# One layer of cross attention finished by the tile, and self attention with its output step moved one pipeline step later

## The chip, the cores and the metric

The kernel runs on one core of one Trainium2 chip. The core has TensorE (PE, matrix products and transposes into PSUM), VectorE (DVE), ScalarE (ACT), GpSimd (POOL) and SyncE (SP, here only for DMAs). Each engine works through its own instructions in order, and they meet through semaphores. The metric is the device time of one execution in microseconds; lower is better. Everything is computed in float32.

## What is computed

A small perceiver of two layers: 128 sequences of 32 latents with 128 features, and a context of 257 rows a sequence. Each layer is a cross attention to the context, a self attention and a mixture of eight experts (two a token), with residuals and norms between. Cut to the parts that the change touches, the reference computes:

```python
# layer 1, cross attention, 16 heads of 8, per sequence
q = z(x) @ Wq.T; k = ctx @ Wk.T; v = ctx @ Wv.T
p = softmax(q k^T / sqrt(128))          # 32 x 257 a head
x = x + (p @ v) @ Wo.T + bo
# self attention of both layers, 16 heads of 8, 32 x 32 scores a head
x = x + (softmax(scores) @ v) @ Wo      # layer 0 relative positions, layer 1 causal with rotary factors
# then a router picks two of eight experts for each token
```

## The kernel before

The work stands in passes, one after another with a barrier between. A tile is 128 tokens, that is 4 sequences (B4) of 32 latents (LEN); there are 32 tiles.

`cross_many_heads` (the second cross attention, semaphores p6) works in units of one sequence, 4 a tile, 128 in all, as a software pipeline: in one step b the engines have several units in hand. For one unit b:

- PE makes the scores (L1493, 4 groups of 4 heads, 257 columns), then in the same step the keys and values of the unit two later (L1501, L1503), the transposes of the probabilities of the unit before (L1514), and for the unit two back the transposes of `spread` (L1533, in `shares`) and the product of values and probabilities (L1540, in `weigh`).
- DVE takes the negated row maxima (L1633, in `largest`), then a copy of the last probability column and the reciprocal of the sums (L1673, L1674), a copy of half the turned probabilities (L1678), and `finish` of the unit three back: `end_ps` times the last value (L1614), plus `o_ps` (L1617), times `share_ps` (L1621), and a sum over the 4 heads of a group into `oT` (L1625). `finish` stands ahead of `largest`.
- ACT makes the exponentials (L1586, four a unit, each with a read of its sum), the copy of keys and values (L1595) and the other half of the turned probabilities (L1602). The next scores wait for the last exponential.
- POOL spreads the last column and the reciprocals over the heads (L1720, 128 x 256), and does the norms and the joining of the experts' results for other tiles.

Softmax has 257 columns; the 257th (`LAST`) is handled apart from the 256 that are turned, with `m.last_values`.

Once a tile, in steps of their own: b=0 the normed input (L287, L1562), b=1 its copy and the query product (L1651, L1564), b=2 the queries (L1656) and the output product (L1567), b=3 the residual (L1664). `joined.dve` ends DVE's step 1 and `tail.dve` its step 3.

`self_attention` serves both layers (p4 relative, p8 causal). Here a step is a whole tile, and step n has tile n - s at stage s: 0 norm and transpose (`zT`), 1 queries and keys, 2 values, 3 scores, sum, maximum, subtraction (POOL L1375) and exponential (ACT L1253), 4 transpose of the probabilities (DVE L1327), the weighted values (PE L1211, here called weigh) and the division (`o`, DVE L1350, L1352), 5 transpose of `o` (PE L1171), its copy (ACT L1234), the output product (PE L1184) and the new X (DVE L1341). `Routing` runs in the same steps with a lag of READY: norms of a group of four tiles (POOL L264), router logits, the choice (DVE L938 to L972), ranks, and the scatter of the rows to the experts' input (POOL L776). STEPS is 32 + AFTER. The order inside a step is written out by hand: PE scores, queries and keys, transpose of `o`, values, output product, transpose of z, router work, weigh; ACT keys and queries, copy of `oT`, `zT`, exponential, copy of the values (`v_all`, L1262), rows for the experts. ACT's copy of the values may overwrite a buffer only when the weighted values of two tiles before are done.

Of the kernel before, what the change touches and what calls it, by code (L numbers as in the profile page):

```python
# [24 lines left out]
P = 128  # L25
# [660 lines left out]
class Routing:  # L686
# [6 lines left out]
    READY = 8  # L693
    AFTER = 18
# [74 lines left out]
    def pool_scatter(self, pool, n, k):  # L769
        m, s = self.m, self.s  # L770
        g, j = self.group_at(n, 9, self.GROUP)
# [107 lines left out]
    def act_slots(self, act, n):  # L879
        s = self.s  # L880
        g, j = self.group_at(n, 9)
# [23 lines left out]
    def dve_logits(self, dve, n, weighed):  # L905
        s = self.s
        g, j = self.group_at(n, 4)
# [66 lines left out]
    def dve_place(self, dve, n, weighed):  # L974
        s = self.s
        g, j = self.group_at(n, 8)
# [90 lines left out]
def self_attention(m, name, relative):  # L1067
# [20 lines left out]
    with ExitStack() as own, nc.Block() as block:  # L1088
# [4 lines left out]
        v_all = sb("v_all", [P, 2, B4 * G, H4, HD + 1])  # L1093
# [45 lines left out]
        def _(pe):  # L1139
            mm = nc.tensor.matmul  # L1140

            def work(n, at):
                t = at(3)
                if t.live:
# [4 lines left out]
                    if t.past(3):  # L1149
                        pe.wait_ge(tail.x_new, t.before(3))  # L1150
# [14 lines left out]
                t = at(5)  # L1165
                if t.live:
                    pe.wait_ge(s["o"], t.nth())
                    if at(1).live:
                        pe.wait_ge(s["zT"], at(1).nth())
                    routing.pe_turned_read(pe, n)  # L1170
                    nc.tensor.transpose(oT_ps, o[:, t.par, :], ident).then_inc(s["oT_ps"], 1)  # L1171
# [7 lines left out]
                t = at(5)  # L1179
                if t.live:  # L1180
                    pe.wait_ge(s["oT"], t.nth())
                    if at(3).live:
                        pe.wait_ge(s["summed"], at(3).nth())
                    mm(y_ps, oT[:, t.par, :], wo, start=True, stop=True).then_inc(s["y_ps"], 1)  # L1184
# [20 lines left out]
                if t.live:  # L1205
                    pe.wait_ge(s["pT"], t.nth())
                    pe.wait_ge(s["v"], t.nth(H4))
                    for b in range(B4):
                        for g in range(G):
                            w, n = H4 * (HD + 1), b * G + g  # L1210
                            last = mm(o_ps[b * LEN:(b + 1) * LEN, g * w:(g + 1) * w],  # L1211
                                      pT[:, t.par, n * LEN:(n + 1) * LEN], v_all[:, t.par, n],
# [6 lines left out]
        def _(act):  # L1219
            def work(n, at):  # L1220
                routing.act_slots(act, n)
                t = at(1)
# [6 lines left out]
                t = at(5)  # L1229
                if t.live:  # L1230
                    act.wait_ge(s["oT_ps"], t.nth())
                    if t.past(2):
                        act.wait_ge(s["y_ps"], t.before(2))
                    nc.scalar.activation(oT[:, t.par, :], oT_ps, ACT.Copy).then_inc(s["oT"], 1)  # L1234
# [19 lines left out]
                t = at(2)  # L1254
                if t.live:
                    act.wait_ge(s["v_ps"], t.nth())
                    act.wait_ge(s["ones"], 3)
                    if t.past(2):
                        act.wait_ge(s["o_ps"], t.before(2))
# [148 lines left out]
def cross_many_heads(m):  # L1408
# [22 lines left out]
    with ExitStack() as own, nc.Block() as block:  # L1431
# [174 lines left out]
        def _(dve):  # L1606
# [29 lines left out]
            def steps(at):  # L1636
                cur, nxt, prev = at(3), at(2), at(4)
                for b in range(B4):
# [6 lines left out]
                    if t.live:  # L1645
                        finish(t, u)
# [423 lines left out]
```

## Time and profile before

| | us |
|---|---|
| median of 3 runs | 1639.16 (1632.37 to 1641.44) |
| the profiled execution | 1640.08 |
| its span in the trace | 1638.1 |

| engine | busy us | share |
|---|---|---|
| PE matmul | 1280.6 | 78% |
| PE weight load | 1107.7 | 68% |
| DVE | 1093.9 | 67% |
| ACT | 840.1 | 51% |
| POOL | 771.2 | 47% |

The busy shares are means over passes with different limits. In time order the passes are: setup and first cross attention to 175 us, relative scores to 207, the first self attention to 466, the first experts to 637, the second cross attention to about 1213, the second self attention to about 1460 with its tables, the second experts and the joining of their results to the end. A row of the timeline gives start, duration, engine, line, operation, output and input, and in square brackets the idle time before it with what ended it. The clock column of the windows is TensorE's granted clock as a share of 2.4 GHz; 0.50 is 1.2 GHz.

### The profile page before, as it was taken

The page shows a single profiled execution, that of the slowest core. Times are in us where ns is not written, and L with a number is a line of the kernel's source. Part 1 is how long each engine was busy: PE and PEld are TensorE (multiplying, and loading weights), DVE is VectorE, ACT ScalarE, POOL GpSimd, SP SyncE. Part 2 cuts the span into 40 slices and gives each one's busy share as a digit, 9 for nine tenths or more (in the row PEclk, how much of TensorE's full clock was granted, in tenths as well). Part 3 has the DMA queues.
Part 4 walks back from the last instruction along what each step waited for, and adds up shares of the span by engine and source line. Part 5 has one row for each costly group of instructions (what it writes and reads, how often), then busy time and mean ns, then how long its engine had stood idle before and what let it go on. Part 6 is the DMA issues. An engine that isn't in the chain of part 4 may idle for free. (4 is left out here: it accounts for less than half of the span.)

```text
span 1638.1 us, 48674 instructions
## 1 busy us (share of the span) xinstructions
PE 1280.6 (78%) x15138; PEld 1107.7 (68%) x15139; DVE 1093.9 (67%) x3599; ACT 840.1 (51%) x2658; POOL 771.2 (47%) x1508
## 2 busy tenths in 40 slices
PE   3878789897659995888888888888869898529991
PEld 2656778786659994666666666666648787529991
DVE  4555377877356663888888888888868977523334
ACT  1554256564224442666666666666646756315440
POOL 2555033767546653444443444444333465646661
PEclk9898588888579997999999999999978989659996
DMA  7997552221122212121111111111000000022225
GB/s 224 254 251 196 207 166 69 60 60 50 36 63 67 63 53 89 60 66 67 32 32 48 32 32 44 36 32 32 27 14 2 10 22 25 32 61 72 68 59 164
DMA packets 91996, 122.00 MB, mean 74 GB/s; under 512 B 12689, under 2 KB 67218, under 8 KB 91858
## 3 DMA queue, kind: packets, MB, share of 16 engines
q1 hardware_dynamic: 74194, 82.77, 17.3%
q0 software_dynamic: 12288, 34.82, 7.3%
q10 hardware_dynamic: 5376, 2.63, 0.5%
q8 instruction: 80, 1.31, 0.3%
q14 instruction: 58, 0.48, 0.1%
HBM read 89.68 MB, written 30.49 MB: 73 GB/s over the span
## 5 line engine op out<-in xcount | busy, mean ns | idle before, releaser
L1586 ACT ACTIVATE p_prob<-six,p_nm 128x257 f32<-128x257 f32 x512 | 235.9, 474 | 187.4 <-DVE p_nm L1633 180.5
L1720 POOL TENSOR_TENSOR p_spread<-p_both,sb_const 128x256 f32<-128x256 f32 x128 | 78.4, 613 | 248.1 <-DVE p_both L1674 190.5
L1633 DVE TENSOR_REDUCE p_nm<-six 128x2 f32<-128x514 f32 x256 | 164.7, 684 | 10.2 <-PE six L1493 4.8
L1493 PE MATMUL six<-p_kv,p_q_all 32*128 32x257 f32 x1024 | 92.2, 426 | 94.7 <-ACT p_prob L1586 94.5
L1823 PE MATMUL bank<-sb_w,m_experts_aT 128*128 x1152 | 155.7, 278 | 6.9 <-ACT m_experts_aT L1852 4.4
L1839 PE MATMUL six<-m_experts_xT,m_experts_w 128*128 128x128 f32 x1152 | 156.0, 279 | 0.1
L1802 POOL DMA_INDIRECT expert_outputs<-m_experts_y,m_experts_dest x144 | 142.6, 990 | 26.1 <-POOL m_experts_tiny L1801 14.7
L1823 PEld LDWEIGHTS bank<-sb_w,m_experts_aT 128*128 128x128 f32 x1152 | 140.4, 192 | 11.9 <-issue 11.7
L776 POOL DMA_INDIRECT expert_inputs<-p_r_x,p_r_slot x128 | 126.2, 986 | 41.6 <-issue 34.0
L1839 PEld LDWEIGHTS six<-m_experts_xT,m_experts_w 128*128 128x128 f32 x1152 | 143.3, 196 | 0.7 <-issue 0.3
L1514 PE MATMUL six<-sb_const,p_prob 128*128 128x128 f32 x1024 | 138.1, 280 | 1.8 <-ACT p_pT L1602 1.6
L1375 POOL TENSOR_TENSOR p_score<-p_score,p_mx 128x512 f32<-128x512 f32 x64 | 67.0, 1048 | 153.4 <-DVE p_mx L1320 151.6
L1493 PEld LDWEIGHTS six<-p_kv,p_q_all 32*128 32x128 f32 x1024 | 43.5, 184 | 124.6 <-issue 124.6
L1514 PEld LDWEIGHTS six<-sb_const,p_prob 128*128 128x128 f32 x1024 | 120.9, 145 | 2.7 <-ACT p_prob L1586 1.8
L1678 DVE COPY p_pT<-six 128x512 f32<-128x512 f32 x128 | 86.4, 675 | 38.7 <-PE six L1514 38.7
L1586 ACT ACTIVATION_READ_ACCUMULATOR p_prob<-six,p_nm 128x1 f32 x512 | 104.0, 203 | 0.0
L1154 PE MATMUL six<-p_kT,p_q_all 32*128 32x32 f32 x2048 | 87.5, 286 | 7.1 <-issue 5.3
L1801 POOL TENSOR_TENSOR m_experts_tiny<-sb_const 128x1 f32<-128x1 f32 x144 | 40.1, 278 | 111.7 <-DVE m_experts_y L1880 59.4
L1501 PE MATMUL bank<-p_ctxT,sb_w_WkT_x 128*128 128x256 f32 x256 | 92.1, 442 | 0.8 <-ACT p_kv L1595 0.8
L1595 ACT ACTIVATE p_kv<-bank 128x512 f32<-128x512 f32 x128 | 77.9, 608 | 24.1 <-PE bank L1503 24.1
L1154 PEld LDWEIGHTS six<-p_kT,p_q_all 32*128 32x128 f32 x2048 | 77.6, 199 | 14.6 <-issue 11.5
L1262 ACT ACTIVATE p_v_all<-bank 32x128 f32<-32x128 f32 x256 | 70.6, 276 | 31.6 <-PE bank L1211 19.3
(282 smaller groups left out, 3404.4 us busy)
## 6 DMA issues: line engine op xcount, KB each, us to landing
ctxN_ring<-ctxN POOLq DMA_DIRECT2D x32, 516.0 KB, 11.3
ctxT_ring<-ctxT SPq DMA_DIRECT2D x32, 514.0 KB, 12.0
p_ctxT<-ctxT SPq DMA_DIRECT2D x32, 514.0 KB, 3.6
m_experts_x<-expert_inputs SPq DMA_DIRECT2D x144, 64.5 KB
bd_scores<-p_rows SPq DMA_DIRECT2D x32, 256.0 KB, 2.8
p_bd<-bd_scores SPq DMA_DIRECT2D x32, 256.0 KB
sb_w<-w SPq DMA_DIRECT2D x32, 256.0 KB
p_y<-expert_outputs SPq DMA_DIRECT2D x32, 128.0 KB, 3.5
```

Of the source, the lines that this page charges most:

```text
L776: m.nc.gpsimd.indirect_dma_start(m.xs_dram[:, :], bass.IndirectOffsetOnAxis(ap=self.slot[:, TOPK * t + k:TOPK * t + k + 1], axis=0), self. ...
L1154: last = mm(quad[:, g, keys], q_all[rows, t.par, b], kT[rows, t.par, keys], start=True, stop=True, tile_position=(32 * g, 0))
L1493: last = mm(scores_ps[:, g, 0:CTX], q_all[rows, t.par, b], kT[rows, t.par, b, :], start=True, stop=True, tile_position=(32 * g, 0))
L1501: mm(ps[6][:, 0:LAST], m.w["WkT_x"][:, :], ctxT[:, t.par, b, 0:LAST], start=True, stop=True)
L1514: last = nc.tensor.transpose(turned_ps[g // 2][:, g % 2, n * P:(n + 1) * P], prob[:, b, g, n * P:(n + 1) * P], ident)
L1586: last = nc.scalar.activation(prob[:, b, g, :], scores_ps[:, g, 0:CTX], ACT.Exp, bias=nm[:, b % 2, g:g + 1], accum_out=total[:, b % 2, g:g ...
L1633: nc.vector.tensor_reduce(nm[:, b % 2, g:g + 2], scores_ps[:, g:g + 2, 0:CTX], AX.X, ALU.max, negate=True).then_inc(s[most], 1)
L1678: nc.vector.tensor_copy(pT[:, u % 2, 2:4], turned_ps[1]).then_inc(s["pT_b"], 1)
L1720: nc.gpsimd.tensor_tensor(spread[:, u % 2], both[:, u % 2].rearrange("p k g -> p (k g)").unsqueeze(2).unsqueeze(3).broadcast_to([P, 2 * G, ...
L1802: nc.gpsimd.indirect_dma_start(m.ys_dram[:, :], bass.IndirectOffsetOnAxis(ap=dest[:, t.par:t.par + 1], axis=0), y[:, t.par, :], None).then ...
L1823: last = nc.tensor.matmul(ps[6 + t.two][:, 0:D], aT[:, t.two, f * P:(f + 1) * P], m.w2[:, DS(held[p] + f * D, D)], start=(f == 0), stop=(f ...
L1839: last = nc.tensor.matmul(ps[2 + t.two][:, f * P:(f + 1) * P], w[:, t.two, f * P:(f + 1) * P], xT[:, t.two, :], start=True, stop=True)
```

## The change

In the cross attention `finish` becomes one copy of `share_ps` and one product `o_ps` times that copy, which goes to a tile-wide buffer `masked`; the sum over the four heads moves to POOL, once a tile, as two additions (`halves`, then `oT`). The 257th column is no longer added on DVE in each unit: POOL makes the spread in two operations (share, then share times the last probabilities), PE sums it over the latents' group with a small product into `end_ps`, DVE multiplies it by the last values once a tile (`end_v`), and a second output product adds it. `finish` now stands first in DVE's step. In the self attentions the transpose of `o`, its copy, the output product and the new X go from stage 5 to stage 6, the division from the end of DVE's step (stage 4) to the start of the next (stage 5); the transpose of `o` stands first in PE's step, its copy first in ACT's; ACT copies the values ahead of `zT` and the exponential, and the values have three buffers. READY and AFTER grow by one.

```diff
@@ Routing
-    READY = 8
-    AFTER = 18
+    READY = 9
+    AFTER = 19
@@ self_attention, buffers
-        v_all = sb("v_all", [P, 2, B4 * G, H4, HD + 1])
+        v_all = sb("v_all", [P, 3, B4 * G, H4, HD + 1])
@@ PE: now first in the step, ahead of the scores (was stage 5, behind queries and keys)
+                t = at(6)
+                if t.live:
+                    pe.wait_ge(s["o"], t.nth())
+                    if at(1).live:
+                        pe.wait_ge(s["zT"], at(1).nth())
+                    routing.pe_turned_read(pe, n)
+                    nc.tensor.transpose(oT_ps, o[:, t.par, :], ident).then_inc(s["oT_ps"], 1)
@@ ACT: copy of oT first; then keys, queries; then the values; then zT, exponential
+                t = at(6)
+                if t.live:
+                    act.wait_ge(s["oT_ps"], t.nth())
...
+                t = at(2)
+                if t.live:
+                    act.wait_ge(s["v_ps"], t.nth())
+                    act.wait_ge(s["ones"], 4)
+                    if t.past(3):
+                        act.wait_ge(s["o_ps"], t.before(3))
@@ DVE: the division at the start of the next step, with dve_logits and dve_place
+                t = at(5)
+                if t.live:
+                    dve.wait_ge(s["o_ps"], t.nth())
...
@@ cross_many_heads, PE
-                for out, first in ((share_ps, 0), (end_ps, G)):
-                    nc.tensor.transpose(out, spread[:, b % 2, first:first + G].rearrange("p g h d -> p (g h d)"), ident)
+                nc.tensor.transpose(share_ps, spread[:, b % 2, 0].rearrange("p g h d -> p (g h d)"), ident)
+                mm(end_ps[:, b * LEN:(b + 1) * LEN], spread[:, b % 2, 1].rearrange("p g h d -> p (g h d)"),
+                   c[:, C_R4:C_R4 + LEN], start=True, stop=True)
...
-                        pe.wait_ge(s["oT"], seq(prev, B4 - 1))
-                        mm(misc_ps, oT[:, prev.par, :], m.w["WoT_x"][:, :], start=True, stop=True).then_inc(s["y_ps"], 1)
+                        pe.wait_ge(s["oT"], prev.nth())
+                        mm(misc_ps, oT[:, prev.par, :], m.w["WoT_x"][:, :], start=True, stop=False)
+                        mm(misc_ps, end_v[:, prev.par, :], m.w["WoT_x"][:, :], start=False, stop=True).then_inc(s["y_ps"], 1)
@@ DVE
-                nc.vector.tensor_scalar(ended[:, :], end_ps, m.last_values[:, n:n + 1] if t.known else ...
-                nc.vector.tensor_tensor(whole[:, :], o_ps, ended[:, :], ALU.add).then_inc(s["whole"], 1)
-                nc.vector.tensor_tensor(shared[:, :], whole[:, :], share_ps, ALU.mult).then_inc(s["shared"], 1)
-                nc.vector.tensor_reduce(oT[:, t.par, b * LEN:(b + 1) * LEN], ...
+                nc.vector.tensor_copy(share[:, b % 2, :], share_ps).then_inc(s["share"], 1)
+                nc.vector.tensor_tensor(masked[:, t.par, :, b * LEN:(b + 1) * LEN], o_ps..., share[:, b % 2, :]..., ALU.mult)
+                    if b == 2 and prev.live:
+                        nc.vector.tensor_tensor(end_v[:, prev.par, :]..., end_ps..., m.last_values[:, prev.cols(B4)]..., ALU.mult)
-                        nc.vector.tensor_copy(both[:, u % 2, 1, :], prob[:, u, :, LAST]).then_inc(s["ends"], 1)
@@ POOL
+                    if b == 2 and prev.live:
+                        pool.wait_ge(s["masked"], seq(prev, B4 - 1))
+                        nc.gpsimd.tensor_tensor(halves[:, :, :], masked[:, prev.par, 0:2, :], masked[:, prev.par, 2:4, :], ALU.add)
+                        pool.wait_ge(s["halves"], prev.nth())
+                        nc.gpsimd.tensor_tensor(oT[:, prev.par, :], halves[:, 0, :], halves[:, 1, :], ALU.add)
-                        nc.gpsimd.tensor_tensor(spread[:, u % 2], both..., mine, ALU.mult).then_inc(s["spread"], 1)
+                        nc.gpsimd.tensor_tensor(spread[:, u % 2, 0], recip..., mine, ALU.mult).then_inc(s["spread_share"], 1)
+                        nc.gpsimd.tensor_tensor(spread[:, u % 2, 1], spread[:, u % 2, 0], prob[:, u, :, LAST]..., ALU.mult)
```

## Rows read from the trace of the kernel before

**Rows 1.** Windows by pass: first self attention, second cross, second self.
```profile
207.00:447.00 240.00, 200.42 (x2770) 182.14 (x2770) 164.97 (x558) 130.36 (x353) 131.60 (x202) 0.78 0.25 74
645.00:1213.00 568.00, 468.42 (x5261) 369.04 (x5257) 486.17 (x1522) 373.02 (x1279) 236.16 (x614) 0.98 0.13 41
1222.00:1416.00 194.00, 167.61 (x2669) 151.47 (x2669) 152.08 (x526) 115.98 (x302) 98.87 (x139) 0.87 0.06 18
```
**Rows 2.** Timeline of one tile of the second cross attention, steps b=0 to b=3.
```profile
906.60 0.72 PE L1493 MATMUL six<-p_kv,p_q_all 32*128 32x257 f32 x8 [0.21 <-ACT p_prob L1586]
907.86 0.35 DVE L1614 TENSOR_SCALAR p_ended<-bank,sb_last_values 128x128 f32<-128x128 f32 x1
...
909.18 1.28 DVE L1633 TENSOR_REDUCE p_nm<-six 128x2 f32<-128x514 f32 x2
...
911.97 0.72 PE L1493 MATMUL six<-p_kv,p_q_all 32*128 32x257 f32 x8 [1.81 <-ACT p_prob L1586]
...
914.67 0.69 DVE L1678 COPY p_pT<-six 128x512 f32<-128x512 f32 x1 [0.48 <-PE six L1514]
...
915.58 0.72 PE L1493 MATMUL six<-p_kv,p_q_all 32*128 32x257 f32 x8
...
917.75 1.28 DVE L1633 TENSOR_REDUCE p_nm<-six 128x2 f32<-128x514 f32 x2
...
920.63 0.72 PE L1493 MATMUL six<-p_kv,p_q_all 32*128 32x257 f32 x8 [1.37 <-ACT p_prob L1586]
```
**Rows 3.** Groups by line: busy us and mean ns of what `finish` does.
```profile
L1617 DVE TENSOR_TENSOR p_whole<-bank,p_ended 128x128 f32<-128x128 f32 x128 | 37.3, 291 | 4.4
L1625 DVE TENSOR_REDUCE p_oT<-p_shared 128x32 f32<-128x128 f32 x128 | 48.4, 378 | 4.4
```
**Rows 4.** Timeline: TensorE with 128 x 128 weights and 32 columns, two passes.
```profile
337.17 0.30 PEld L835 LDWEIGHTS bank<-p_r_both,sb_const 128*128 128x128 f32 x2
...
337.39 0.30 PEld L836 LDWEIGHTS bank<-p_r_sums,sb_const 128*128 128x128 f32 x2
```
**Rows 5.** Timeline of POOL in the same tile, and TensorE at its shares.
```profile
912.28 0.61 POOL L1720 TENSOR_TENSOR p_spread<-p_both,sb_const 128x256 f32<-128x256 f32 x1
...
912.85 0.46 POOL L1714 TENSOR_TENSOR p_xb<-sb_X,sb_bX 128x128 f32<-128x128 f32 x1
...
914.47 0.38 PE L1533 MATMUL bank<-sb_const,p_spread 128*128 128x128 f32 x2
```
**Rows 6.** Timeline of a step of the first self attention ahead of the routing.
```profile
237.19 1.09 PE L1154 MATMUL six<-p_kT,p_q_all 32*128 32x32 f32 x32
...
238.88 1.06 PE L1177 MATMUL bank<-sb_w_Wv_a,p_zT 128*128 128x128 f32 x8
...
240.45 0.78 ACT L1242 ACTIVATE p_zT<-six,sb_cols 128x512 f32<-128x512 f32 x1 [0.69 <-PE six L1191]
...
241.31 1.09 PE L1154 MATMUL six<-p_kT,p_q_all 32*128 32x32 f32 x32
```
**Rows 7.** Timeline of the first self attention, where POOL first makes norms of a group.
```profile
246.22 1.00 DVE L287 TENSOR_SCALAR p_z<-sb_X,sb_MEAN,sb_RN 128x128 f32<-128x128 f32 x1
...
247.17 0.63 ACT L1253 ACTIVATE p_prob<-p_score 128x512 f32<-128x512 f32 x1 [1.83 <-POOL p_score L1375]
247.70 1.17 ACT L1262 ACTIVATE p_v_all<-bank 32x128 f32<-32x128 f32 x4
...
248.93 2.08 PE L1177 MATMUL bank<-sb_w_Wv_a,p_zT 128*128 128x128 f32 x8 [1.66 <-ACT p_v_all L1262]
```
**Rows 8.** Waits of TensorE, 240 to 420 us (engine, line, waited for: us, times, longest).
```profile
PE six L1171 <- DVE p_o L1352: 9.2, 7, 3.5
PE six L1184 <- ACT p_oT L1234: 7.2, 7, 4.0
```
**Rows 9.** Waits of TensorE in the second self attention, 1240 to 1415 us.
```profile
PE six L1171 <- DVE p_o L1352: 5.0, 9, 2.0
```
**Rows 10.** Timeline: clearing `v_all` at the start of the first self attention.
```profile
205.91 1.02 DVE L1285 MEMSET p_v_all<- 128x1152 f32 x1 [5.36 <-PEq L1970]
```

More of the change, by code:

```diff
@@ L975, in dve_place @@
         s = self.s
[L976 removed]
+        g, j = self.group_at(n, 9)
         if g is None:
@@ L1253, in work @@
                     nc.scalar.activation(prob[:, t.par, :], score[:, t.par, :], ACT.Exp, scale=scale).then_inc(s["probs"], 1)
[L1254 to L1259, printed above, removed]
[L1260 to L1264 removed]
                 routing.act_rows(act, n)
[L1266 removed]
+                t = at(4)
                 if t.live and not relative:
@@ L1419, in cross_many_heads @@
         "z", "zT_ps", "zT", "q_ps", "q", "kv_ps", "kv", "k_end", "scores", "most_a", "most_b", "exp_b", "pT_ps",
-        "pT_a", "pT_b", "recip", "ends", "spread", "o_ps", "ended", "whole", "shared", "oT", "y_ps", "xb", "weighted")}
+        "pT_a", "pT_b", "recip", "spread_share", "spread", "o_ps", "share", "masked", "end_v",
+        "halves", "oT", "y_ps", "xb", "weighted")}
     ctx_in = [m.sem("p6_ctx_in_a"), m.sem("p6_ctx_in_b")]
@@ L1441, in cross_many_heads @@
         nm, total = (sb(n, [P, 2, G]) for n in ("nm", "total"))
-        both = sb("both", [P, 2, 2, G])
-        spread = sb("spread", [P, 2, 2 * G, H4, HD])
-        ended, whole, shared = (sb(n, [P, P]) for n in ("ended", "whole", "shared"))
+        recip = sb("recip", [P, 2, G])
+        spread = sb("spread", [P, 2, 2, G, H4, HD])
+        share, masked, halves = sb("share", [P, 2, P]), sb("masked", [P, 2, H4, P]), sb("halves", [P, 2, P])
+        end_v = sb("end_v", [P, 2, P])
         y = sb("y", [P, 2, TOPK * D])
@@ L1521, in bank_read @@
                 if t.live:
-                    pe.wait_ge(s["shared"], seq(t, u))
+                    pe.wait_ge(s["masked"], seq(t, u))
                 if b == 1 and at(2).live:
@@ L1526, in bank_read @@
                     pe.wait_ge(s["q"], at(2).nth())
+                if b == 2 and at(4).live:
+                    pe.wait_ge(s["end_v"], at(4).nth())
                 if b == 3 and at(4).live:
@@ L1638, in steps @@
                 for b in range(B4):
+                    t, u = near(at, b, -3)
+                    if t.live:
+                        take_share(t, u)
+                        finish(t, u)
+                    if b == 2 and prev.live:
+                        if prev.past(2):
+                            dve.wait_ge(s["y_ps"], prev.before(2))
+                        nc.vector.tensor_tensor(
+                            end_v[:, prev.par, :].rearrange("p (b i) -> p b i", b=B4), end_ps.rearrange("p (b i) -> p b i", b=B4),
+                            m.last_values[:, prev.cols(B4)].unsqueeze(2).broadcast_to([P, B4, LEN]),
+                            ALU.mult).then_inc(s["end_v"], 1)
                     if b == 0 and nxt.live:
```

123 lines of the change are left out of this document (56 added, 67 removed).

## The prediction

> **What bounds the kernel now.** I read the windows by pass first [rows 1]. The second cross attention takes 568 us at a granted clock of 0.98, and DVE is busy 486.2 of them (86%), PE 468.4 and ACT 373.0. The self attentions take 240 and 194 us with clocks of 0.78 and 0.87: there TensorE spends a part of its time at 1.2 GHz, and DVE is busy 69% and 78%. The change touches only these three passes; all that it does must show in their 1002 us.
>
> Then the timeline of one tile of the cross attention [rows 2]. The reader is to see the start of the scores of each unit: 906.60, 911.97, 915.58, 920.63. Two steps are short (b=1: 915.58 - 911.97 = 3.61) and two are long (b=0: 5.37, b=2: 5.05). A short step is a ring of three engines: scores on PE, 0.78 until DVE starts the maxima, 0.7 to 0.8 until ACT's first exponential, four exponentials with their sums, next scores. From the start of the maxima to the next scores it is 2.79 (909.18 to 911.97) and 2.88 (917.75 to 920.63), I take 2.85. So no step is under 0.78 + 2.85 = 3.63. A long step is one in which DVE comes to its maxima late: at b=0 they start 909.18, 2.58 behind the scores and not 0.78, so 1.80 late; at b=2 they start 2.17 behind, 1.39 late. What DVE does in that time is `finish` (907.86 to 909.18, 1.32) and, at b=2, the queries. PE waits 1.81 and 1.37 in those places for the exponentials. The pass is bound by DVE's order in two steps of four and by the ring in the other two.
>
> In the self attentions an early step shows 4.12 from scores to scores (237.19 to 241.31) [rows 6]. PE is busy nearly all of it, and DVE is too: sum, maximum, transpose, queries and the rest. From 247 on, POOL's norms of a group delay the subtraction, ACT waits 1.83 for it, the copy of the values stands behind the exponential in ACT's order, and PE waits 1.66 for that copy; behind it the same products run at the low clock level (2.08 for what was 1.06) [rows 6, 7].
>
> **The cross attention, part by part.** `finish` is 1.32 from start to next start: L1614, then 291 ns, a like product, and 378 ns with gaps of 0.04 [rows 2, 3]. The new one is a copy of 128 x 128 out of PSUM and a product of PSUM with SBUF. The copy isn't in the trace; the nearest rows are the 128 x 128 operations with one PSUM input, 0.29 to 0.35 [rows 2, 3], and it can't be below nothing since it takes DVE's slot. I take 0.29 + 0.29 and two gaps, 0.62. Saved: 0.70 in each unit. The two operations ahead of `finish` at b=0 change places with it; their sum is the same. `end_v` adds one product of 128 x 128 at b=2, 0.29 + 0.04 = 0.33 [rows 3]. The dropped copy of the last column is short and stands where DVE waits for PE anyway (0.48 at 914.67) [rows 2]: nothing.
>
> Where it counts: at b=0 the lateness is 1.80 and falls by 0.70. At b=2 it is 1.39 and falls by 0.70 - 0.33 = 0.37. At b=1 and b=3 DVE was in time, the ring sets the step, and the saving there buys idle time: nothing. Sum for a tile 1.07, for 32 tiles 34 us; I take 33, since at the first and last tiles the pipeline isn't full. The stall that is next late is DVE again: at b=0 `tail.dve`, `finish` and the norm still come 1.1 late, at b=2 the queries 1.0.
>
> PE gets dearer. A transposed share was one pass of two; the small product is two passes of 128 x 128 weights and 32 columns, 0.22 together (337.17 to 337.39) [rows 4], in the place of one pass, 0.11: 0.11 more a unit. It could cost between 0 and 0.22. PE waited 0.21 at the end of a short step (at 906.60) [rows 2], so it needs about 3.45 of one and 3.56 now, still under the ring's 3.63; the second output product adds two passes, 0.22, at b=2, which has 0.8 to spare. On the path: 0, at the bad end 0.11 x 64 short steps = 7 us.
>
> POOL takes over the head sum: 128 x 256 (0.61) and 128 x 128 (0.46) with a gap of 0.17, 1.24 a tile, behind a wait for the last `masked` of the tile before; behind that wait stand the spread of unit 1 and `joined.pool`. The old `finish` of step 2 ended about 1.57 behind the scores (maxima at 2.17 less some 0.60 for the queries), the new one at 0.87; POOL is then done at 2.2, and PE asks for `oT` 2.50 + 0.33 behind its scores: 0.6 of cover. The spread of a unit goes from 0.61 to 0.46 + 0.17 + 0.46 = 1.09 [rows 5]. The late one is that of unit 3: POOL starts it at 912.28, 5.68 behind the scores of b=0, because the norms and the joined results stand ahead. It would end at 913.37. TensorE asked for it at 914.47, 2.50 into step 1; with step 0 shorter by 0.70 it asks at 913.77. Cover 0.4; without it every tile loses what is missing.
>
> A rule that speaks against this: POOL and DVE get in each other's way. In the trace DVE's norm took 1.00 at 246.22 and ended with POOL's subtraction of 1.05 [rows 7]; elsewhere it takes about a third. The Trainium skill (SBUF — State Buffer, on the shared port pair) says that VectorE and GpSimd hold one pair of ports exclusively, for VectorE where it has two SBUF inputs or runs in a two-port mode, and the loser waits for the whole instruction. By that rule the 2.7 more of POOL a tile could catch the norm at b=0 once more in six tiles, at about 0.3 each, 2 us in all; the new DVE operations read PSUM and would not be caught. The sum leaves it out.
>
> **The self attentions, part by part.** DVE's stream doesn't change: the division at the end of step n and at the start of step n+1 are the same place, router operations included. What changes is PE's and ACT's.
> - Gone are PE's waits for `o` and `oT`: 9.2 + 7.2 in the first, 5.0 in the second [rows 8, 9], and waits for the copy of the values such as the 1.66 [rows 7]. About 24 us of PE time. DVE sets much of the pace, and its 69 and 78% with the same order leave room for about half: -12 us. Bounds 0 and -24.
> - New is the order of ACT: values (1.17) ahead of `zT` (0.78), and the transpose of `o`, first in PE's step and ahead of the scores, waits for `zT`. In the early step the values' product ends at 239.94; then 1.17 and 0.78 and two hand-overs of 0.05 give 241.99, and the scores that started at 241.31 start 0.7 later [rows 6]. That price holds in steps where PE is ahead, from step 6 until DVE's choice of experts makes DVE the later one, about 5 steps in the first pass; in the second the copy is shorter and DVE's step longer, 0.4. Together 5.5 us. Its cover in the routed steps is DVE's work; without it it costs in all steps (below).
> - One more step in each pass. It adds an early step of 4.12 [rows 6] and makes a full one into a light one; I take 2.5 each, 5 us; bounds 0 and 4.12 each. The queue of SP has no more in it, and POOL's scatters only come a step later.
> - Clearing three buffers and not two: 1.02 becomes 1.53 by size, and one more small copy; ahead of the first norm, so PE waits for it [rows 10]. 0.8 each, 1.6 us.
> Sum: -12 + 5.5 + 5 + 1.6 = 0.
>
> **The sum.** Against the profiled execution of 1640.1 (span 1638.1, 2.0 around it): 1640.1 - 33 + 0 = 1607.1. The median of the runs shown is 0.9 lower than that execution, and I predict 1606.
>
> **The rivals.**
> 1. The self attentions gain much more: the stalls go and with them the low clock. At 1.2 GHz eight passes of the values took 2.08 against 1.06 [rows 6, 7]. If all 24 us of waits go and a tenth of the 434 us of the two passes goes from the low to the high level in PE-bound work, a further 0.1 x 434 x 0.2 = 9: 1606 - 12 - 9 = 1585. For it: mean clocks of 0.78 and 0.87. Against: DVE's unchanged stream, and the late subtraction that starts the stalls stays on POOL. The Trainium skill (TensorE: Matmul & The Clock Gate, on oscillation) says that gaps between groups of products make the clock fall; by it fewer gaps give this result, and the row of 2.08 behind a wait of 1.66 agrees.
> 2. POOL's spread or the denser PE is late in the cross attention: each tile loses 0.3, 10 us: 1616.
> 3. The change doesn't do what it says: DVE's time goes into waits for `o_ps` and shares, and only b=2 gains, 0.37 x 32 = 12: 1639 - 12 = 1627.
> 4. Slower: PE's wait for `zT` in front of the scores decides every step of the self attentions, since the sum on DVE starts right when the scores end. 0.7 x 32 + 0.4 x 32 = 35, with the new step and the clearing 42, nothing gained: +42 - 33 = +9; and if the idle 0.7 in 4.8 brings the low level in 4 more steps of each pass, at 1.02 for the values alone and some 2.5 for all of PE's products, +20 more: 1639 + 29 = 1668. It decides from the point where DVE's routed step is shorter than PE's with the wait, about 5.2. Against it: routed steps carry DVE's choice, about 1.1 more.
>
> **How the numbers follow.** The forecast 0.50, rival 1 0.17, rival 2 0.13, rival 3 0.11, rival 4 0.09. The forecast's own range, from the bounds of the self attentions (-12 to +12) and of PE's price (+7), is 1594 to 1622. For 8 in 10 the range must reach into rivals 1 and 3: 1587 to 1628. About 0.5% (8 us) is what a measurement of this kernel can tell from no change; faster than that is under 1631. Faster: the forecast, 1, 2 and most of 3, 0.83. Same: the rest of 3 and the near end of 4, 0.09. Slower 0.08.
>
> **What would show it.** In the changed profile the cross attention should take about 535 us; scores at b=0 and b=2 should still be late by 1.1 and 1.0, the short steps stay 3.6; a wait of PE's share transposes for POOL would be rival 2, one of DVE's share copy for `o_ps` at b=0 rival 3. In the self attentions the waits of L1171 and L1184 should be gone, an early step should read about 4.8 with PE waiting for `zT`, and a routed step under 6.7. If the clock there falls under 0.78 and 0.87, rival 4 is at work; if it rises over 0.9, rival 1. The prediction fails above all if the self attentions move by more than 15 us.

## The result and the profile after

The changed kernel takes 1579.0 us (median, 1575.8 to 1587.3) beside 1636.3 for the kernel before on the same chip: ratio 0.9667, 95% interval 0.9639 to 0.9695. The forecast was 1606 with a range down to 1587, so the change gave 57 us where 33 were expected. Timed again in two later groups, the whole change came to 0.9657 (0.9639 to 0.9676) and 0.9728 (0.9679 to 0.9778).

Windows from the first to the last result of each changed pass (residual written by DVE, 32 of them). Columns: stretch, length, busy time and instructions of PE, PE's weight loads, DVE, ACT and POOL, granted clock, DMA share, GB/s. Before: first self attention, second cross attention, second self attention.

```profile
228.53:415.64 187.11, 161.74 (x2474) 145.84 (x2470) 144.20 (x476) 110.23 (x305) 107.96 (x171) 0.84 0.24 72
672.56:1212.63 540.07, 444.38 (x5013) 350.55 (x5013) 463.42 (x1455) 352.12 (x1210) 228.23 (x595) 0.98 0.13 39
1242.00:1416.29 174.29, 148.98 (x2464) 134.66 (x2459) 140.87 (x503) 107.06 (x280) 95.13 (x135) 0.90 0.06 18
```

The same three after the change:

```profile
227.99:405.98 177.99, 144.75 (x2405) 130.64 (x2401) 135.63 (x469) 107.04 (x295) 105.36 (x168) 0.88 0.23 70
662.77:1151.19 488.42, 451.87 (x5206) 364.48 (x5201) 379.51 (x1119) 352.63 (x1211) 289.21 (x781) 1.00 0.14 43
1182.66:1349.24 166.58, 136.31 (x2387) 122.31 (x2382) 136.19 (x495) 99.88 (x271) 92.60 (x132) 0.93 0.06 18
```

The cross attention lost 51.7 us (540.07 to 488.42) and its clock rose from 0.98 to 1.00. The self attentions lost 9.1 and 7.7 in these stretches, but the time ahead of their first results doesn't count in them and grew. The two spans are 1638.1 and 1574.0. Of the 12 us of their difference that are not in the cross attention, some 6 lie ahead of the first self attention, in code that is the same in both, and are the scatter of single executions.

The timeline of a tile after, scores and maxima, answers to [rows 2]:

```profile
889.84 0.72 PE L1497 MATMUL six<-p_kv,p_q_all 32*128 32x257 f32 x8 [0.18 <-ACT p_prob L1594]
890.04 0.29 DVE L1621 COPY p_share<-bank 128x128 f32<-128x128 f32 x1
890.37 0.29 DVE L1627 TENSOR_TENSOR p_masked<-bank,p_share 128x128 f32<-128x128 f32 x1
890.66 0.35 DVE L287 TENSOR_SCALAR p_z<-sb_X,sb_MEAN,sb_RZ 128x128 f32 x1
890.92 1.29 DVE L1636 TENSOR_REDUCE p_nm<-six 128x2 f32<-128x514 f32 x2
...
897.50 0.72 PE L1497 MATMUL six<-p_kv,p_q_all 32*128 32x257 f32 x8
897.65 0.29 DVE L1621 COPY p_share<-bank 128x128 f32<-128x128 f32 x1
897.97 0.29 DVE L1627 TENSOR_TENSOR p_masked<-bank,p_share 128x128 f32<-128x128 f32 x1
898.18 0.28 DVE L1649 TENSOR_TENSOR p_end_v<-bank,sb_last_values 128x128 f32<-128x128 f32 x1
898.38 0.68 DVE L1667 TENSOR_TENSOR p_q_all<-bank,sb_const 128x512 f32<-128x512 f32 x1
898.98 1.28 DVE L1636 TENSOR_REDUCE p_nm<-six 128x2 f32<-128x514 f32 x2
```

At b=0 the maxima stand 1.08 behind the scores, at b=2 1.48 behind (2.17 in [rows 2]). The durations, the second column of numbers, matter less than the distances between starts: from the share's copy to the product it is 0.32, and the product waits for the copy; from there to `end_v` it is 0.21 and to the queries 0.20, and these wait for nothing just made, although each copy or product shows 0.28 to 0.29 as its length.

The loop's body holds two tiles, so every other tile starts with a loop trip, and there DVE waits 0.45 for issue ahead of the share's copy (at 906.25). The tile above has no such trip; that of [rows 2] has one. In the next tile, which has one too and so compares with [rows 2], the maxima are 1.83 behind at b=0 (2.58 before):

```profile
905.52 0.80 PE L1497 MATMUL six<-p_kv,p_q_all 32*128 32x257 f32 x8 [0.17 <-ACT p_prob L1594]
...
907.35 1.29 DVE L1636 TENSOR_REDUCE p_nm<-six 128x2 f32<-128x514 f32 x2
```

So tiles alternate. The results show that, and a third kind in the kernel before (DVE's residual write, three tiles in a row):

```profile
706.15 0.28 DVE L1664 TENSOR_TENSOR sb_X<-bank,p_xb 128x128 f32 x1
723.53 0.28 DVE L1664 TENSOR_TENSOR sb_X<-bank,p_xb 128x128 f32 x1
742.81 0.28 DVE L1664 TENSOR_TENSOR sb_X<-bank,p_xb 128x128 f32 x1
760.08 0.28 DVE L1664 TENSOR_TENSOR sb_X<-bank,p_xb 128x128 f32 x1
```

The tiles before are 17.27 and 17.70 long in turn, but six of the 31 distances (here 723.53 to 742.81) are 19.28 to 19.37. After, all are 15.75 and 16.30. (The first and last few differ in both kernels, since the pipeline fills and drains there.) What happens in the long ones is in the timeline and the windows of the kernel before:

```profile
732.12 0.72 PE L1493 MATMUL six<-p_kv,p_q_all 32*128 32x257 f32 x8 [1.85 <-ACT p_prob L1586]
...
734.48 1.91 PE L1514 MATMUL six<-sb_const,p_prob 128*128 128x128 f32 x8
...
736.43 0.69 DVE L1678 COPY p_pT<-six 128x512 f32<-128x512 f32 x1 [2.09 <-PE six L1514]
```

```profile
733.30:736.30 3.00, 3.00 (x15) 2.91 (x14) 1.04 (x4) 2.42 (x9) 1.05 (x3) 0.50 0.26 23
736.50:739.50 3.00, 3.00 (x39) 2.30 (x38) 2.77 (x10) 0.53 (x1) 0.00 (x0) 1.00 0.97 361
```

Behind PE's wait of 1.85 the granted clock is 0.50 (1.2 GHz), from 733.0 to 736.4, and then 1.00 (2.4 GHz) again. The eight transposes of the probabilities take 1.91 where they take 1.04 in the other tiles, DVE waits 2.09 for them, and the tile is 1.6 longer than the 17.70 of its kind. I had seen the wait of 1.81 in [rows 2] and a mean clock of 0.98 in [rows 1], and made nothing of either.

### The profile page after: what moved, and what is told of

It reads as the page before. It is cut to its first block and busy times, and to the rows that moved or that the text cites. A ratio compares the mean times of both kernels' runs of the same rounds, so it can differ in the third digit from the quotient of the medians.

```text
span 1574.0 us, 48807 instructions
## 1 busy us (share of the span) xinstructions
PE 1252.2 (80%) x15330; PEld 1089.4 (69%) x15331; DVE 999.9 (64%) x3249; ACT 836.8 (53%) x2658; POOL 833.9 (53%) x1700
## 5 line engine op out<-in xcount | busy, mean ns | idle before, releaser
L1844 PEld LDWEIGHTS bank<-sb_w,m_experts_aT 128*128 128x128 f32 x1152 | 141.1, 193 | 10.5 <-issue 10.1
L1518 PE MATMUL six<-sb_const,p_prob 128*128 128x128 f32 x1024 | 132.8, 273 | 1.8 <-ACT p_pT L1610 1.5
L1518 PEld LDWEIGHTS six<-sb_const,p_prob 128*128 128x128 f32 x1024 | 116.0, 141 | 2.7 <-ACT p_prob L1594 1.8
L1737 POOL TENSOR_TENSOR p_spread<-p_recip,sb_const 128x128 f32<-128x128 f32 x128 | 51.3, 401 | 86.5 <-DVE p_recip L1684 86.3
L1880 ACT ACTIVATE m_experts_xT<-six 128x128 f32<-128x128 f32 x144 | 39.1, 272 | 89.2 <-PE six L1852 74.4
L1873 ACT ACTIVATE m_experts_aT<-m_experts_h 128x512 f32<-128x512 f32 x72 | 45.5, 632 | 76.4 <-DVE m_experts_h L1918 43.8
```

The lines of the kernel that those rows point to most:

```text
L1518: last = nc.tensor.transpose(turned_ps[g // 2][:, g % 2, n * P:(n + 1) * P], prob[:, b, g, n * P:(n + 1) * P], ident)
L1844: last = nc.tensor.matmul(ps[6 + t.two][:, 0:D], aT[:, t.two, f * P:(f + 1) * P], m.w2[:, DS(held[p] + f * D, D)], start=(f == 0), stop=(f ...
```

## The experiments

Five groups ran, on four chips; those on VectorE's price and on the wait for `zT` shared one. Within a group all kernels share one chip and its own runs of the kernel before (its median is given), so ratios are compared. "Pass" is the time from the first to the last result of the second cross attention; it hardly depends on the chip (487.7 to 488.8 with the changed cross attention wherever it ran), so it is compared across groups too.

**The halves of the change.** One kernel takes only the hunks of the cross attention, one only the hunks of the self attentions and the router's due times (`READY`, `AFTER`, the group steps). Kernel before: 1587.1.

> The kernel before with the change of the cross attention alone, the self attentions as they were. Theory A: the cross attention's term was mis-sized and is all of the gain but a little: 50 to 55 us less than before, ratio 0.967 to 0.970, pass about 528 us. Rival B: the term of 33 us was right and the rest comes from the self attentions (a higher clock, stalls gone): 33 us less, ratio 0.980.

Measured: 0.9684 (0.9632 to 0.9737), pass 487.7, tiles 15.74 and 16.30. Theory A: the cross attention alone gives 50 us. The 528 expected for the pass was wrong.

> The kernel before with the change of the self attentions (and their router's due times) alone. Theory A: the two passes are 2 and 4 us shorter as in the trace of after: 6 us less, ratio 0.996. Rival B: 18 to 20 us less, ratio 0.988. The prediction's own term was 0.

Measured: 1.0050 (1.0026 to 1.0074). Both theories missed: the self attentions' part costs 8 us. Its trace shows early steps of 5.03 and 4.95 where they are 4.12 and 4.30 without it.

**The place of `finish` alone.** In `steps` of the kernel before:

```diff
+                    t, u = near(at, b, -3)
+                    if t.live:
+                        finish(t, u)
                     if b == 0 and nxt.live:
                         dve.wait_ge(joined.pool_step, nxt.nth(joined.steps))
                         ...
-                    t, u = near(at, b, -3)
-                    if t.live:
-                        finish(t, u)
```

> The kernel before; only, in the first of a tile's four steps of the cross attention, VectorE finishes the older unit ahead of the norm, no longer behind it. Theory A (the place is worth something by itself): the wait of 0.66 ahead of the norm (at 727.65) is filled with the finish. 0.6 in each second tile and 0.1 in the others is 11 us; if PE's wait of 1.85 then is too short to bring the low clock in every fourth tile, 13 us more: ratio 0.985 to 0.993. Rival C (only the cheaper operations count): 0 to 2 us, ratio 0.999 to 1.000, tile periods 17.3, 17.7, 17.3, 19.4 as before.

Measured: 1.0015 (0.9987 to 1.0043), tiles of 17.19 and 17.67, four of 19.28 to 19.33, pass 535.1. Rival C: the place is worth 0.06 a tile. The wait for issue is not filled but moves along: it now stands ahead of `finish`.

```profile
911.61 0.18 DVE L201 BATCH_NORM_AGGREGATE sb_mv<-sb_bnst 128x2 f32<-128x6 f32 x1
912.35 0.35 DVE L1614 TENSOR_SCALAR p_ended<-bank,sb_last_values 128x128 f32<-128x128 f32 x1 [0.56 <-issue]
```

**Filling TensorE's wait.** The kernel before with twice the value products in two of four steps:

```diff
-                for n in range(2):
+                for n in [0, 1] * times:
                     for g in range(G):
                         last = mm(o_ps[32 * g:32 * g + 32, :], ...
...
-                        weigh(t, u)
+                        weigh(t, u, 2 if b in (0, 2) else 1)
```

> The kernel before; only, TensorE does the sixteen value products of a unit twice in the first and third of a tile's four steps (0.65 more each, into what is its wait of 1.85 and 1.37; the result is the same). Theory A (each fourth tile is 1.7 to 2.1 longer because TensorE's clock falls to half for 4 us behind a long wait): the fourth tiles lose it, 8 x 1.7 = 13 us less though TensorE does 42 us more: ratio 0.992, granted clock 1.00 all through the pass. Rival D (the fourth tile is long for another reason, in VectorE's order or the loop's end): the periods stay, 0 to 10 us more, ratio 1.000 to 1.006.

Measured: 0.9989 (0.9959 to 1.0020), pass 533.0. The windows of 700 to 1150 us, first of this kernel, then of the one with `finish` moved (whose clock shows the falls):

```profile
700.00:1150.00 450.00, 392.68 (x5080) 313.65 (x5082) 394.04 (x1238) 300.22 (x1033) 196.16 (x513) 1.00 0.13 38
```

```profile
700.00:1150.00 450.00, 372.36 (x4209) 294.18 (x4208) 389.62 (x1223) 297.22 (x1020) 194.48 (x509) 0.98 0.13 38
```

No tile of 19.3 is left, the clock is 1.00, and the tiles stay 17.27 and 17.70 although TensorE does sixteen products more in two steps. TensorE's longest wait for the exponentials fell from 1.8 to 1.4. So the long tiles are the low clock behind the long wait: theory A for the mechanism. The size was too large: this chip had five long tiles in the kernel with the old cross attention (the self attentions' half above, pass 538.0), not eight, and the 5 us by which this pass is shorter are below what the total can tell: its interval leaves out theory A's 0.992 and reaches rival D's range, so the mechanism rests on the trace alone.

**VectorE's price.** On the cross attention's half, further copies whose result nobody reads, in two of four steps. Kernel before: 1627.0.

```diff
                         take_share(t, u)
+                        if b in (0, 2):
+                            for k in range(2):
+                                nc.vector.tensor_copy(pad[:, k, :], share_ps)
                         finish(t, u)
```

> The cross attention changed alone, with two further copies of the share into a buffer that nobody reads, behind the share's copy in the first and third of a tile's four steps. Theory A (VectorE's late steps carry every ns, but an operation that depends on nothing just before it costs its start interval of 0.20, as the products at 897.97 and 898.18 show, and the masked product no longer waits for the copy): 3 x 0.20 - 0.33 = 0.27 a step, 0.54 a tile, 17 us more than with the change alone, ratio to before 0.979. Rival P (the prediction's price of 0.33 for every operation): 1.32 a tile, 41 us, ratio 0.994.

Measured: 0.9752 (0.9713 to 0.9790), pass 499.4, 11.7 more than without (487.7 in the first group); tiles 16.19 and 16.56. That is under both, nearer theory A's 17 than rival P's 41.

The chained kernel adds `.then_inc(padded[b][k], 1)` to each copy and `dve.wait_ge(padded[b][k], t.nth())` behind it.

> The same two copies in the same places, but each is waited for before the next operation starts, as the four operations of the old finish were. Theory A: 0.20 + 0.33 + 0.33 - 0.33 = 0.53 a step, 1.06 a tile, 33 us more than with the change alone, ratio 0.989, so 16 us more than without the waits. Rival P: the same as without the waits.

Measured: 0.9891 (0.9845 to 0.9937), pass 520.4, 32.7 more than without, theory A's 33; tiles 16.72 and 17.41. The timelines, unchained and chained:

```profile
904.82 0.29 DVE L1620 COPY p_share<-bank 128x128 f32<-128x128 f32 x1
905.03 0.48 DVE L1646 COPY p_pad<-bank 128x128 f32<-128x128 f32 x2
905.43 0.28 DVE L1626 TENSOR_TENSOR p_masked<-bank,p_share 128x128 f32<-128x128 f32 x1
```

```profile
901.68 0.29 DVE L1621 COPY p_share<-bank 128x128 f32<-128x128 f32 x1
901.88 0.60 DVE L1647 COPY p_pad<-bank 128x128 f32<-128x128 f32 x2
902.52 0.29 DVE L1627 TENSOR_TENSOR p_masked<-bank,p_share 128x128 f32<-128x128 f32 x1
```

Two copies take 0.40 from start to the next start without waits and 0.64 with them. The same work costs 21 us more in the pass when each operation waits for the one before. Neither copy reads what the other wrote, so it is the semaphore and its wait that cost here, not the data. The Trainium skill (VectorE: DVE Perf Modes, "The DRAIN you can't avoid") says that the pipe empties after each operation whether or not there is a wait, and that semaphores between copies cost nothing. The traces don't agree for these 128 x 128 operations (0.64 with the waits, 0.40 without), and the measurement decides. Another sentence of the same section, that a next operation which is not held starts earlier, does agree.

The third kernel has the copies at `b in (1, 3)`.

> The two unchained copies in the second and fourth of a tile's steps, where VectorE waits 0.31 and 0.67 for TensorE's share and 0.20 and 0.22 for the scores. Theory A (there the ring of scores, maxima and exponentials sets the step): 0 to 3 us more than with the change alone, ratio 0.968 to 0.970. Rival V (VectorE's sum of work sets the tile wherever it lies): 17 us as in the other steps, ratio 0.979.

Measured: 0.9713 (0.9649 to 0.9777), pass 487.9, tiles 15.67 and 16.36: nothing, theory A. Of the prediction's picture this holds: in the short steps the ring sets the pace and DVE's work there is free.

The fourth has four copies at `b in (0, 2)`.

> Four unchained copies in the first and third steps. Theory A: 5 x 0.20 - 0.33 = 0.67 a step, 1.34 a tile, 42 us, ratio 0.994, tile periods 17.1 and 17.6; TensorE's waits for the exponentials grow by 0.67 to some 1.5, and whether that brings the low clock in every fourth tile again tells from which wait on it comes: with it 8 to 10 us more, ratio 1.000, without it 0.994.

Measured: 0.9928 (0.9900 to 0.9956), pass 523.9, 36.2 more than without (42 were expected); tiles 16.99 and 17.30, clock 1.00, none long. Against the kernel with two copies in the same steps, four more copies a tile cost 24.5 us, 0.19 each: here the price of 0.20 holds. TensorE's longest wait for the exponentials between 700 and 1150 us, in this kernel and in the kernel before:

```profile
PE six L1496 <- ACT p_prob L1593: 57.5, 80, 1.4
```

```profile
PE six L1493 <- ACT p_prob L1586: 78.4, 76, 1.8
```

No low level followed waits of up to 1.4 in these 450 us. Waits of 1.8 came in every other tile, the low level behind at most every second of them, in four to six of 31 tiles; which of them it follows was not tested.

**The wait for `zT` in the self attentions.** On the changed kernel, and beside it. Kernel before: 1632.5. The first edit puts ACT's block that copies the values behind its block that makes `zT`; the second puts PE's block that transposes `o` behind its scores, queries and keys, where the kernel before had it:

```diff
                 t = at(6)
-                if t.live:        # first in PE's step
-                    pe.wait_ge(s["o"], t.nth())
-                    ...
                 t = at(3)
                 ...
                     mm(k_ps, wk, zT4[:, t.par, :, 0, :], start=True, stop=True).then_inc(s["qk_ps"], 1)
+                t = at(6)
+                if t.live:
+                    pe.wait_ge(s["o"], t.nth())
+                    ...
```

> The changed kernel itself, as the reference of this group. Theory A: the cross attention gives 50 to 52 us here too; the self attentions give between +8 (as alone, 1.005 of before) and -7 (as in the first profiles), so 0.967 to 0.974 of before.

Measured: 0.9657 (0.9639 to 0.9676), 1577.3 us, pass 488.3, the ratio just under the expected band.

> The changed kernel; only, in the self attentions ScalarE makes zT before it copies the values. Theory A (the early steps of 5.04 and 4.95 are TensorE's wait of 0.63 for zT behind the copy of 1.2): early steps 4.4 or less, 0.63 in 7 to 13 steps of each pass, 9 to 16 us less than the changed kernel. Rival S (the later copy of the values holds TensorE's next values' product or its use of them, as the stall of 1.66 in the kernel before): the early gain is given back in the routed steps, 0 to 5 us less.

Measured: 0.9579 (0.9561 to 0.9596), 14.0 us less; early steps 4.38.

> The changed kernel; only, TensorE transposes o behind the scores and the products of the queries and keys, where it stood before, no longer first in the step. Theory A (what waits for zT in front of the scores is that transpose alone): scores start 0.6 earlier, the products of the queries wait for zT beside the scores of 1.0: early steps 4.4, 9 to 16 us less than the changed kernel. Rival S: oT comes later for the last product and the gain is lost there, 0 us.

Measured: 0.9558 (0.9533 to 0.9583), 15.8 us less; early steps 4.11 and 4.30, the pace of the kernel before.

> Both of these edits together. Theory A: they remove the same wait, so together no more than 0.3 a step beyond one alone: early steps 4.1 to 4.4, 10 to 18 us less than the changed kernel, 0.956 to 0.961 of before.

Measured: 0.9568 (0.9549 to 0.9587), 14.0 us less, nothing beyond one alone. Theory A in all three: the wait at the head of the step, which either edit takes away. Rival S fell.

The traces show a second wait at the moved transpose. TensorE's waits in the first self attention of the changed kernel (228 to 406 us):

```profile
PE six L1186 <- DVE p_score L1329: 10.1, 11, 1.7
PE six L1149 <- ACT p_zT L1255: 3.1, 5, 0.6
PE six L1149 <- ACT p_r_zT L866: 1.7, 3, 0.7
```

`p_r_zT` is ScalarE's copy of the router's turned rows, behind `zT` in its order; the transpose of `o` waits for it too (L1149), 1.7 us here and 3.7 in the second pass.

The step of the changed kernel, scores to scores 5.04 (TensorE's timeline):

```profile
234.15 0.30 PE L1149 MATMUL six<-sb_const,p_o 128*128 128x128 f32 x1 [0.63 <-ACT p_zT L1255]
234.39 1.09 PE L1161 MATMUL six<-p_kT,p_q_all 32*128 32x32 f32 x32
...
239.43 1.09 PE L1161 MATMUL six<-p_kT,p_q_all 32*128 32x32 f32 x32
```

With the transpose late, 4.11:

```profile
239.43 1.09 PE L1154 MATMUL six<-p_kT,p_q_all 32*128 32x32 f32 x32
...
243.54 0.65 PE L1154 MATMUL six<-p_kT,p_q_all 32*128 32x32 f32 x16
```

**The halves again.** The first profiles had the self attentions shorter, the half alone was slower; the chips differ in the routed steps. Kernel before: 1629.7.

> The self attentions' change alone once more. Theory R (its worth hangs on how slow the routed steps are): beside a kernel before of 1625 to 1640, with routed steps of 6.0 to 7.1, ratio 0.994 to 0.998 (3 to 9 us less); beside one of 1587, with routed steps of 5.2, 1.005 as before. Rival N (no gain anywhere, the first pair of profiles was noise): 1.000 to 1.006 in either case.

Measured: 1.0043 (1.0019 to 1.0066). The last 15 steps of its second self attention took 6.0 in the mean (5.2 in this half's trace of the first group), and the half still cost 7 us: theory R fell, rival N holds.

> The cross attention's change alone once more. Both theories: 50 to 52 us less than before, ratio 0.968 to 0.970; the second cross attention's results stand 15.74 and 16.30 apart as on the first chip. With theory R the whole change (0.966) is the product of the two halves beside a slow kernel before.

Measured: 0.9716 (0.9691 to 0.9741), pass 488.4, a little less gain than expected. The product with the self half is 0.9758, 1% above what the whole gave where the kernel before had this pace (0.9657, 0.9667). So all went on one chip. Kernel before: 1590.1.

> The changed kernel, on one chip with its two halves. Theory N (the self attentions' part costs 5 to 8 us in whatever kernel): 0.003 to 0.005 above the cross attention alone in ratio to before. Theory I (the halves help one another, or the whole's code lies better): 0.003 to 0.008 below it.

Measured: 0.9728 (0.9679 to 0.9778), 1547.0 us.

> The cross attention's change alone on the same chip. Theory N: 0.968 to 0.970, below the changed kernel. Theory I: 0.970 to 0.972, above it.

Measured: 0.9707 (0.9667 to 0.9747), 1542.2 us.

> The self attentions' change alone on the same chip: 1.004 to 1.005 by both theories.

Measured: 1.0053 (1.0029 to 1.0078), 1599.4 us.

> The changed kernel with the transpose of o behind the scores and the queries and keys, on the same chip: 14 to 16 us below the changed kernel again, ratio to it 0.990, which is 0.004 to 0.007 below the cross attention alone if theory N holds.

Measured: 0.9608 (0.9572 to 0.9645), 1527.7 us: 19.3 below the changed kernel, where 14 to 16 were expected, and by ratio 0.010 below the cross attention alone, where 0.004 to 0.007 were. So the self attentions' half without this one reordering gains some 15 us; with it, it costs 5. This kernel has the lowest median on both chips on which it ran, though on the first the other two edits are within 2 us of it.

On one chip the halves do multiply (0.9707 x 1.0053 = 0.9758, inside the whole's interval), and the whole is 4.8 us over the cross attention alone, as theory N says, though the two intervals overlap. Whether the halves help each other on the chips where the kernel before takes 1630 stays open: there the whole and its halves were never side by side.

Where the self half's cost lies is seen in the last group. First the cross attention alone, then the changed kernel: up to the first result of the first self attention, that pass, and the second pass, by windows.

```profile
0.00:224.85 224.85, 157.65 (x2142) 126.69 (x2144) 111.55 (x477) 89.73 (x306) 80.90 (x206) 0.83 0.78 221
224.85:403.65 178.80, 151.52 (x2474) 137.70 (x2470) 143.86 (x477) 109.57 (x305) 108.07 (x171) 0.86 0.25 75
1163.48:1318.21 154.73, 134.81 (x2464) 121.87 (x2459) 140.49 (x503) 106.11 (x280) 95.30 (x135) 0.96 0.06 20
```

```profile
0.00:230.19 230.19, 156.98 (x2219) 126.00 (x2221) 115.49 (x485) 93.54 (x317) 81.95 (x207) 0.85 0.77 219
230.19:401.59 171.40, 142.98 (x2405) 130.36 (x2402) 136.38 (x469) 106.43 (x295) 104.93 (x168) 0.88 0.24 73
1168.59:1324.54 155.95, 135.14 (x2407) 122.05 (x2407) 137.66 (x494) 99.79 (x274) 91.07 (x130) 0.94 0.06 18
```

The first result comes 5.3 later, the first pass is then 7.4 shorter, the second 1.2 longer. Between the cross attention's last result and the second pass's first one lie 26.4 and 31.7, again 5.3, and behind the last result 218.9 and 222.1, 3.2 more. The sum is 7.6 us; with 1.9 more between the first pass and the cross attention it is the 9.5 by which the two spans differ. The medians differ by 4.8, so single pieces of 1 or 2 us can be scatter; the two of 5.3 come back in the other pairs.

## Why the prediction was right or wrong

**The sign and the place were right, the cross attention's term was mis-sized.** -33 was forecast, -51.7 measured in the pass, -46 to -50 in total by the half alone. Of the 18.7 missing in the pass about 10 are a low clock that the sum had at nothing, and about 7 the price of two operations at b=2; both are worked out below. The term was 1.07 a tile. Against its own kind of tile (17.70, with the loop trip) the measured one is 1.40, against the other kind 1.52, 1.46 in the mean. By steps, in the tile with the trip: b=0 from 5.37 to 4.63, 0.74 where I had 0.70; b=2 from 5.05 to 4.35, 0.70 where I had 0.37; b=1 0.11 longer. In the other kind b=0 falls from 4.83 to 3.94 and b=2 from 5.11 to 4.36.

- The step that failed is the price of `finish` and `end_v` at b=2. I charged every operation its length and a gap, 0.62 and 0.33. What stands behind the new ones doesn't wait for them, and they cost 0.53 (897.65 to 898.18) and 0.20 (898.18 to 898.38), 0.22 less a tile, 7 us in 31 tiles. Of the 0.70 in that step 1.32 - 0.53 - 0.20 = 0.59 is this. The rest, 0.11, I put down to DVE reaching the step earlier, which is argued and not shown.
- That the price hangs on the waits of a chain is shown by the two kernels with copies: 11.7 us unchained, 32.7 chained.
- I took one tile for all. It was the kind with the loop trip, in which b=0 gains 0.74; in the other kind it gains 0.89.
- Missing altogether was the low clock. Six long tiles at some 1.65 are 10 us of the 51.7; the rest, 41.7 over 31 tiles, is 1.35 a tile, less than 1.46 because the first and last tiles gain less. TensorE's wait for the exponentials no longer passes 1.0 after the change, and no fall followed waits of 1.4 in the kernel with four copies.

**The ring, the share's cover, the place.** Short steps stayed 3.66 to 3.72, and extra DVE work there cost nothing: right. TensorE showed no wait for POOL's spread, so the share's cover held. PE's price of the small product did show, 0.06 to 0.11 at b=1, within the bound I gave. The change of place was right at nothing, 0.06 a tile. The lateness at b=0, predicted 1.1, is 1.05 in the kind of tile I took and 0.30 in the other; at b=2, predicted 1.0, it is 0.70. The 2 us that the prediction left out of its sum, for POOL meeting DVE's norm, didn't come: no norm in the cross attention (L287) took over 0.35, before or after, with 61 us more of POOL's work, 1.9 a tile. (The 2.7 of the prediction isn't the sum of its own terms, 1.24 + 4 x 0.48 = 3.2.) The upper end of the forecast's own range, 1622, should be 1625 by its bounds (1606 + 12 + 7); nothing hangs on it.

**The self attentions: 0 forecast, 7 to 9 us slower measured alone, 5 inside the whole.** The wait for `zT` was right in place and low in size: early steps 5.04 and 4.95, not 4.8 and 4.7, and taking it away gives 14 to 19 us where I had 5.5, since it acts in more than five steps of each pass: further on in the first pass, steps of 5.31, 4.99 and 4.99 become 4.65, 4.20 and 4.27 with the transpose late. The step that failed beside it is "one more step each" at 2.5: the first result of each pass comes 5.3 later (0.5 of it the larger clearing, 1.50 for 1.02), and 3.2 follow behind the last. The waits for `o` and `oT` were to go and fell in part. In the first pass of the first pair `o` went from 9.2 to 1.6 and `oT` from 7.2 to 3.7, but the output product then waits 10.1 for DVE's sum (L1186 above), which it did not before; on the last chip `oT` stays at 9.3 of 10.1. The first pass became 7.4 shorter there, the second 1.2 longer. By an estimate the gain that I put at 12 was 17 to 25 us: what the half cost (8 alone in the first group, 5 inside the whole), less 14 to 19 for the wait and 11 for the two late first results. So the 0 came near the measured loss by luck: three terms were too small and nearly cancelled. In the first pair of profiles what is left for these passes is 6 us shorter, which would have borne the term out; the half run alone, three times, showed the other sign.

**The rivals.** Rival 1 gave a time near the one measured, for the wrong pass: the clock did matter, in the cross attention. Rival 2 (POOL or a denser PE late) didn't come: of POOL's `oT` one wait shows, 2.2 us. Rival 3 fell with b=0. Rival 4's wait is real and acts past the early steps, but doesn't decide the late routed ones, and the cost was 5 to 9 us, not 42.

## What to carry to other kernels

Price a VectorE operation by the distance to the next start in a row of the trace, once for a chain of waits and once for work without them: 0.32 against 0.20 for the same copy here. Before taking one tile as the pattern, list the lengths of all of them: tiles of a third kind and a mean clock of 0.98 were in the profile before, and a window of 3 us on one of them shows the low clock. Time the halves of a change apart: one half here hid a loss of 5 to 9 us, and undoing one reordering in it made the fastest kernel, 0.956 to 0.961 of before.

## What the runs showed of the hardware

- TensorE's clock fell to 0.50, from 733.0 to 736.4 in the first such tile, behind a wait of 1.85; it did so in four to six of 31 tiles, and not between 700 and 1150 us of kernels whose longest wait there was 1.4. Sixteen products more in two steps took the fall away and left the other tiles at 17.27 and 17.70. The Trainium skill (TensorE: Matmul & The Clock Gate, on psum-queue depth-cycling) tells of small idles between groups of products that make the clock oscillate; the trace agrees, with six falls to 0.50 in the pass of the kernel before.
- Two 128 x 128 copies out of PSUM on VectorE took 0.40 to the next start without waits and 0.64 with a wait behind each.
- Chips differ by 3% on the same kernel (medians of the kernel before from 1587 to 1636). The last 15 steps of the second self attention, unchanged, take 5.2 in the mean in the first group's trace of the cross attention alone, and 6.4 in that of the kernel before; there TensorE waits for issue inside its scores, below. The cause was not tested.

```profile
1330.97 0.85 PE L1154 MATMUL six<-p_kT,p_q_all 32*128 32x32 f32 x15
...
1332.23 0.43 PE L1154 MATMUL six<-p_kT,p_q_all 32*128 32x32 f32 x5 [0.40 <-issue]
...
1332.94 0.65 PE L1154 MATMUL six<-p_kT,p_q_all 32*128 32x32 f32 x12 [0.29 <-issue]
```
